# Six loads of a channel-mixing kernel, each issued as a transfer over 120 partitions and one over 8

## The reference

```python
xn  = group_norm(x, 32 groups)                 # 16 channels each
y1  = bn_relu(conv over H (256 taps) of xn)    # (2, 512, 1, 256)
y2  = bn_relu(conv over W (256 taps) of xn)    # (2, 512, 256, 1)
dot = einsum('bck,bck->cb', y1, y2).reshape(b, c)
p   = softmax((dot @ lw1.T + lb1) @ lw2.T + lb2)
out = x + xn * p[:, :, None, None]
```

## Time and profile before

| | us |
|---|---|
| median of 3 runs | 1733.38 (1731.59 to 1733.71) |
| the profiled execution | 1734.45 |
| its span, first to last instruction | 1732.0 |
| busy: DVE, ACT, PE, POOL | 929.8, 664.3, 541.1, 337.0 |

### The profile page before, as it was taken

One profiled execution on the slowest core, in us unless ns is written; L12 is line 12 of the kernel. 1 busy time (PEld: TensorE's weight loads), 2 busy tenths in 40 slices (PEclk: granted clock), 3 DMA queues, 4 the chain that ended last, 5 costly groups with the idle time before them and its releaser, 6 DMA issues.

```text
span 1732.0 us, 14834 instructions
## 1 busy us (share of the span) xinstructions
PE 541.1 (31%) x4306; PEld 224.3 (13%) x4306; DVE 929.8 (54%) x4104; ACT 664.3 (38%) x507; POOL 337.0 (19%) x472
## 2 busy tenths in 40 slices
PE   4588756544243433343344344420000000000000
PEld 1133212112111211111112122210000000000000
DVE  5899999956455665555566556752222222222220
ACT  4688887854454455444554455600000000000000
POOL 7678887820000000000000000000000000000000
PEclk8899978876566655656666566655555555555555
DMA  9999999979999999999999979999999999999999
GB/s 393 426 426 427 402 422 426 427 300 417 433 429 429 429 431 430 430 429 429 430 429 429 431 309 428 430 370 430 430 430 432 432 431 430 431 433 431 431 430 403
DMA packets 52290, 726.12 MB, mean 419 GB/s; under 512 B 6257, under 2 KB 6769, under 8 KB 8050
## 3 DMA queue, kind: packets, MB, share of 16 engines
q1 hardware_dynamic: 34066, 460.94, 62.7%
q10 hardware_dynamic: 18144, 264.25, 35.8%
HBM read 456.73 MB, written 268.44 MB: 419 GB/s over the span
## 4 chain that ended last, share of the span: by engine, by line
DMA 53%; another core or an unknown queue 26%; DVE 8%; ACT 4%; PE 4%; issue 1%; SPq 1%; POOL 0%; ACTq 0%; POOLq 0%; DVEq 0%
DMA xs<-in_x 47%; DVE mul_junk L895 6%; DMA out<-xs 5%; ACT sq_junk L708 2%; DVE xs L969 1%; DMA z<-in_w 1%; PE ps_part L503 1%; ACT xs L775 1%; SPq L328 1%; PE ps_l L616 0%; PE ps_l L604 0%; ACT z L760 0%; PE ps_y L531 0%; PE ps_y L624 0%
## 5 line engine op out<-in xcount | busy, mean ns | idle before, releaser
L895 DVE SCALAR_TENSOR_TENSOR mul_junk<-xs,ps_w 128x256 fp8e5<-128x256 f32 x1856 | 643.2, 417 | 298.2 <-DMA xs<-in_x 295.4
L708 ACT ACTIVATE sq_junk<-xs 128x4096 fp8e5<-128x4096 f32 x128 | 463.3, 3620 | 282.4 <-DMA xs<-in_x 274.5
L969 DVE TENSOR_SCALAR xs<-xs,scale,shift 128x4096 f32<-128x4096 f32 x95 | 227.2, 2412 | 400.7 <-DMA xs<-in_x 400.1
L518 PE MATMUL ps_part<-xs,taps 128*32 128x256 f32 x2048 | 221.3, 608 | 426.3 <-DMA xs<-in_x 426.3
L503 PE MATMUL ps_part<-xs,taps 128*32 128x512 f32 x1024 | 151.6, 739 | 111.9 <-DMA xs<-in_x 108.1
L775 ACT ACTIVATE xs<-xs,shift,scale 128x4096 f32<-128x4096 f32 x33 | 125.4, 3801 | 120.2 <-DMA xs<-in_x 113.4
L518 PEld LDWEIGHTS ps_part<-xs,taps 128*32 128x32 f32 x2048 | 93.1, 164 | 535.3 <-issue 361.6
L417 POOL TENSOR_TENSOR rstd_b<-var,minus_half 128x1 f32<-128x1 f32 (+1 forms) x36 | 20.5, 568 | 715.9 <-DVE var L919 715.9
L895 DVE DVE_READ_ACCUMULATOR mul_junk<-xs,ps_w 128x1 f32 x1856 | 154.6, 83 | 0.0
L388 POOL TENSOR_TENSOR prod<-xs,w_copy 128x768 f32<-128x768 f32 x64 | 116.5, 1826 | 59.7 <-DMA xs<-in_x 57.0
L503 PEld LDWEIGHTS ps_part<-xs,taps 128*32 128x32 f32 x1024 | 42.7, 131 | 210.9 <-issue 209.8
(11 more groups left out here) (105 smaller groups left out, 339.2 us busy)
## 6 DMA issues: line engine op xcount, KB each, us to landing
xs<-in_x SPq DMA_DIRECT2D x215, 2048.0 KB, 27.7
out<-xs ACTq DMA_DIRECT2D x126, 2048.0 KB, 32.9
xs<-in_lw SPq DMA_DIRECT2D x2, 2048.0 KB, 21.0
out<-xs SPq DMA_DIRECT2D x2, 2048.0 KB, 10.7
w_c<-in_w_rows SPq DMA_DIRECT2D x1, 512.0 KB, 3.9
w_sb<-in_w SPq DMA_DIRECT2D x1, 512.0 KB, 9.0
z<-in_w SPq DMA_DIRECT2D x1, 512.0 KB, 23.2
affine_in<-in_g SPq DMA_DIRECT2D x2, 16.0 KB
```

The lines of the kernel that those rows point to most:

```text
L518: last = nc.tensor.matmul(ps_part[b][32 * a:32 * a + 32, 0:W], taps[:, g % 2, hf * JH + j, :], xs[:, s, j * W:(j + 1) * W], start=(hf == 0 ...
L708: nc.scalar.activation(sq_junk[:], xs[:, s, :], ACT.Square, accum_out=sq_sum[:, u % 2, u // 2, b:b + 1], saturate=False).then_inc(squared, 1)
L895: last = nc.vector.scalar_tensor_tensor(out=mul_junk[:, sets[0] % 2, j - first, :], in0=xs[:, s, j * W:(j + 1) * W], scalar=1.0, saturate= ...
L969: return nc.vector.tensor_scalar(xs[:, s, :], xs[:, s, :], scale[:, b, g:g + 1], shift[:, b, g:g + 1], ALU.mult, ALU.add)
```

## The change

Six of the loads, those of the first image's units 9 and 19 (first stage) and 36, 44, 52 and 60 (second stage), are issued as two transfers, one of partitions 0 to 119 and one of partitions 120 to 127. Both raise the slot's semaphore by 16, and `landed` counts both, so every reader still waits for the whole tile. Nothing else differs, and the bytes moved are the same.

```diff
+FIFTEEN = 15 * 8
+IN_TWO = {("x", u, 0) for u in (9, 19, 36, 44, 52, 60)}
...
+def parts_of(key):
+    if key in IN_TWO:
+        return (slice(0, FIFTEEN), slice(FIFTEEN, P))
+    return (slice(0, P),)
+
+
 def landed(slot, key):
-    return 16 * (LOADS[slot].index(key) + 1)
+    return 16 * sum(len(parts_of(k)) for k in LOADS[slot][:LOADS[slot].index(key) + 1])
...
-                sp.dma_start(xs[:, s, :], x_v[u // 2, :, b, part_of(u)]).then_inc(x_loaded[s], 16)
+                for rows in parts_of(("x", u, b)):
+                    sp.dma_start(xs[rows, s, :], x_v[u // 2, rows, b, part_of(u)]).then_inc(x_loaded[s], 16)
```

## The result

The changed kernel takes 1768.33 us (median of 6 runs, 1766.06 to 1770.79) against 1732.62 us for the kernel before (6 runs in all, 1731.59 to 1733.71). The ratio is 1.0206, 95% interval 1.0196 to 1.0217: slower by 35.7 us. The profiled execution is the fastest of the six, 1766.06 us with a span of 1763.6, 31.6 us above that of before (1732.0).

The account below looks back on a forecast made before the run. Bound: the DMA engines' rate, with one late engine setting the first two stages. Profiled 1734.45 us plus 6 x 0.61 = 3.7 gives 1738.1, in terms of the median 1737.1 us, 0.21% slower; range 1731 to 1765.

Parts of the forecast that it names:

- What bounds the kernel: Whole kernel: the DMA engines' rate, 427 to 431 GB/s; in the first two stages, one engine moving its share.
- the late engine: First two stages: one DMA engine is behind, never waits before a stage's end, and works alone for about 7 us.
- The late engine is one of the eight: In the six split loads: the engine that is behind moves nine rows instead of eight, +3.7 us on the path.
- The rule on engines 7 and 15: Skill page saying these are usually slower; by it, relief had about an even chance against the extra row.
- The relief: In the split loads: the engine that is behind is left out, 13 to 18 us faster, 1718 us; chance 0.15.
- The step 6 x 0.61 = 3.7 us: Six split loads: six extra rows at 0.61 us each on the engine that is behind, all on the path.
- SP's issues hidden: On SP: six more issues at 0.33 us lie under queued transfers; 2.0 us at most if that cover is gone.
- I take nothing for the sum: Split loads: 120 and 8 rows move at the even rate, nothing added; upper end 33 us for six.
- the rival with 0.32: Split loads: engines share ways into the partitions, 16.5 + 3.7 = 20 us slower, 1753.6 us; chance 0.32.
- The late engine meets the others' traffic only part of the time: Split loads: reason for taking half of the shared ways' upper bound, 16.5 us.
- the full bound: Split loads with shared ways: each engine at half rate, 5.5 us a load, 33 us for six, giving 1770 us.

Follow-up runs that it names:

- the extra stores: Five extra stores of a constant among the first stage's loads, against the kernel before: on 16 engines 1.0037, 15 and 8 1.0032, 7 1.0039, 4 1.0036, 2 0.9997.

## Why the prediction was wrong

**What bounds the kernel: right.** The steady rate, the late engine's continuous work, and the landing at the first stage's end as the place where a loss shows all held: 19.3 us at that landing and some 13 us more by the end of the second stage (on the chain, the seven scalings that open the third stage end at 1194.2 us instead of 1161.9) make 32.4 us, of which 31.6 are left at the end of the profiled execution. That the late engine never waits is borne out by the packet records.

**The late engine is one of the eight: right.** It was chosen on a reading that had no row; the extra stores show it, and narrow it to two, if the sets lie within one another. The rule on engines 7 and 15 that the prediction set against it ("DMA: Bandwidth & Descriptors" of the Trainium skill, Latency and other measured facts) is tied by that page to transfers whose descriptors are written in software; here all queues of data are hardware queues, so it was no ground for an even chance. The relief, the rival with 0.15, could not happen. The step 6 x 0.61 = 3.7 us can't be read from the change's total, but the stores show that such work lands on the path in full: some 6.4 us put in, 6.6 to 7.5 at the landing.

**SP's issues hidden: right** (split by columns, 1.0000).

**The step that failed is "I take nothing for the sum"**, for the rate of 120 and 8 rows. The reason given, that the nearest rows stay within 1% of each other, compared whole loads with whole loads and said nothing on other forms. Measured in its place: a packet of the 120 rows takes 1.27 us instead of 0.61, one of rows 120 to 127 takes 2.41, and a split costs 10 us in the first stage and 4 in the second, 35.7 us for six where the sum had 3.7. This was the rival with 0.32, and the rule that the prediction named for it ("SBUF — State Buffer" of the Trainium skill, Door 1: The DMA port swizzle) fits in most: rows 120 to 127 fall into two of its groups of four and run at a quarter, rows 0 to 63 reach half of its ports and run at half, and eight rows four apart are each in a port of their own and run at the full rate. For the 120 rows, which carry most of the price, it is not enough: by its table they reach all sixteen ports, and yet ran at half. Which engine writes which rows, and when, must come into it, and no view here shows that. Its further sentence, that only one transfer over all 128 reaches all ports, does not hold here: the even rows alone ran at 431 GB/s.

**The rival's size was halved for a wrong reason.** "The late engine meets the others' traffic only part of the time" fits where stores share the time (3.1 and 4 us a split), but in the first stage all is loads, and the split of unit 9 slowed some 14 us of traffic, its neighbours included. The range then left out the full bound and ended at 1765. That the full bound, 1770, comes close to the 1768.3 measured is in part luck: 5.5 us a load was too low for the first stage (10) and too high for the second (4).

**What stays open:** what makes the third or fourth engine late (the fetching of instructions was not varied); whether the engines wait at the partitions or in main memory; and the 1.5 to 3.6 us by which a split in the first stage costs more here than among loads alone. The packet records narrow the last of these: around unit 9 the packets of the run with that split alone take 8.3 us longer for each of the sixteen engines in the mean, and the stage's last landing moved by 11.3. So the late engine lost more than the mean.

## What to carry to other kernels

A transfer that covers only part of the 128 partitions should be priced by which partitions it covers: contiguous blocks were moved at a half or a quarter of the rate here, with the DMA engines busy, and the loss spread to whole transfers beside them. The sign in a profile is a DMA share near 1 with GB/s well below the steady value; an idle engine would lower both. To find out whether a set of engines holds the late one, give it a few microseconds of extra work and look at one landing.

## What was unexpected of the hardware

- 64 even partitions load at 431 GB/s, 64 contiguous ones at 206, with all sixteen engines busy in both (share 1.01).
- Rows 0 to 119 load at 201 GB/s (packets of 1.27 us instead of 0.61), rows 120 to 127 at 53 GB/s with eight engines busy (2.41 us).
- A split of a load into 120 and 8 rows costs 10 us among the loads of the first stage and 3.1 us where loads and stores alternate.
- One DMA engine of the first stage is behind the others by some 8 us, and of the sets tried, four engines hold it and two do not.
